# A token, scan and expert tower on one core: gathers into two PSUM banks a batch ahead, products of the powers spread over later batches, and another split of u among engines

## The chip, the cores and the metric

The kernel runs on one core of one Trainium2 chip. The metric is the device time in microseconds of one execution. The chip's engines work side by side, each through its own queue in order: TensorE (PE; its weight loads are shown apart as PEld) multiplies matrices into the eight banks of PSUM, VectorE (DVE) and ScalarE (ACT) read and write PSUM and SBUF, GpSimd (POOL) reads and writes SBUF only, and SyncE (SP) issues most of the DMAs. An engine waits for another through semaphores.

## The reference

Eight sequences of 512 ids go through three layers. The first looks every id up in a quantised table of 125 rows, applies a convolution of two taps along the sequence and a relu:

```
e = w_emb[clip(y, 0)];  h = relu(conv(pad(e), w, taps=2))
```

The second adds to h a linear recurrence over the normalised h (called u), with a 64x64 matrix A in four heads, written in the reference as an associative scan in log space; the states are divided by the largest of their row and go through C, and u through D:

```
u = layernorm(h);  x[t] = A x[t-1] + B u[t];  y = (e^2 * x / max|x|) C + u D;  h = h + y
```

The third is a layer norm, one matrix (attn_w), fc1, gelu, fc2, a last matrix and a gelu, with eight experts given by position:

```
x_attn = normed @ attn_w.T + attn_b + xf;  out = gelu(fc2(gelu(fc1(x_attn))) @ next_w.T + next_b);  h = h + out
```

## The kernel before

A batch is one sequence, 512 columns, held as 16 places in a chunk by 32 chunks, so that the scan is 16 steps inside chunks and a scan over the 32 chunks. Eight batches make two groups of four; the scan works on a group at a time.

The front is a loop over b = 0 to 9 that each engine writes out in its own order; all that the change touches lies in it. What it does for batch b:

- `spread_ids(b)` on TensorE copies the row of ids to all partitions of a bank; VectorE's `one_hot(b)` compares it with the row number; GpSimd's `edge(b)` copies the 31 columns at the chunks' edges, `onehot<-onehot` (L465).
- `gather(b)` (L1026 to L1038) is 16 matmuls of one-hot by table into bank 2, in four quarters; only the last quarter waits for `edge(b)`. From batch 1 on it waits for `h_ready` of the batch before, which frees the bank.
- ScalarE writes `h` of the batch from the bank with a relu (L590). VectorE takes its statistics, `st` and `mv` (L745, L749). GpSimd makes `rstd1` and `shift1` of them in four operations of which each waits for the one before (L480 to L483).
- The division (h - mean) * rstd gives `u`, in four pieces of 128 columns. `U_DVE` says how many of them VectorE does (L772); ScalarE does the others (L607). On both this stands one turn of the loop later than the batch's `h`.
- `transpose_u` on TensorE (L1047, four matmuls into bank 3) stands two turns later, and ScalarE's copy to `uT` (L595).

Beside it run the products of the powers of A. The list `prep` has seventeen of them, numbered 0 to 16; each is a matmul into bank 4 or 5 in turn (L986) and a copy by ScalarE (L555) to `pw`, `pw_t`, `late_b`, `pk` or `pk_t`, and most need the copy of the one or two before. `PREP_ROUND` says how many are issued in each turn: first ahead of the turn's transposition, then behind it.

In turns 6 and 7 the first group's run products come in, `run_piece(0, n)`: four of them into bank 6 (L1061, in turn 6) from `uT` of batches 0 to 3, and four into bank 7 (L1067, in turn 7) in three parts each, which need high and low parts of u. The high parts are ScalarE's `late_p`, `b_p` and four `u_first` (L579 to L582, the function `split_high`), the low parts are VectorE's (L755, L778, L779). ScalarE copies each four to `X` (L569). In turn 8 TensorE begins the scan over chunks with `ends` (L1080). Later work (the scan's carries, the mixer, the experts) follows in a written order that the change leaves alone.

Of the kernel before, what the change touches and what calls it, by code (L numbers as in the profile page):

```python
# [37 lines left out]
ACT = mybir.ActivationFunctionType  # L38
# [6 lines left out]
P = 128  # L45
NB = 8
# [4 lines left out]
GB = NB // NG  # L51
# [3 lines left out]
CH = 128  # L55
# [14 lines left out]
RUN = 4  # L70
# [4 lines left out]
OH_SLOTS = 4  # L75
# [15 lines left out]
PA, PA_N = spans(PA_COLS)  # L91
# [3 lines left out]
def build(nc, ids, emb, conv, pack_a, pack_b, fc1, fc2, out):  # L95
    with ExitStack() as ctx:
# [7 lines left out]
        pa = sb("pa", [P, PA_N])  # L104
# [15 lines left out]
        onehot = sb("onehot", [VOC, OH_SLOTS, EXT * NCH], BF16)  # L120
# [13 lines left out]
        scale_h = sb("scale_h", [P, 1])  # L134
        h = sb("h", [P, NB, NQ * CH])
# [37 lines left out]
        with ExitStack() as early:  # L173
# [13 lines left out]
            late_p = sb_early("late_p", [P, 2, (RUN - 1) * P], F32R)  # L187
            b_p = sb_early("b_p", [P, 2, NP * P], F32R)
# [5 lines left out]
        bank = [ctx.enter_context(nc.psum_tensor(f"bank{n}", [P, 512], F32)) for n in range(8)]  # L194
# [9 lines left out]
        scale_h_ready, oh_edge = sem("scale_h_ready"), sem("oh_edge")  # L204
# [6 lines left out]
        idb_done, oh_ready, gat_done, h_ready = sem("idb_done"), sem("oh_ready"), sem("gat_done"), sem("h_ready")  # L211
# [22 lines left out]
        b_hi, b_lo = sem("b_hi"), sem("b_lo")  # L234
# [15 lines left out]
        def late(a):  # L250
            return late_b[:, a].rearrange("p n m -> p (n m)")
# [60 lines left out]
        def ids_bank(b):  # L312
            return bank[{2: 3, 3: 6}.get(b, b % 2)][0:VOC, :]

        def scan_bank(a):
            return bank[6 + a][:]

# [3 lines left out]

        U_DVE = (2, 2, 2, 2, 2, 4, 4, 4)

        PREP_ROUND = ((1, 0), (1, 0), (1, 0), (1, 1), (1, 1), (1, 2), (1, 1), (1, 1), (1, 1), (1, 0))

        FUSED_FRONT = 3
        MIXER = 8
# [16 lines left out]

        assert sum(map(sum, PREP_ROUND)) == N_POW

        def prep_tasks(b, after):
            first = sum(map(sum, PREP_ROUND[:b])) + (PREP_ROUND[b][0] if after else 0)  # L350
            return range(first, first + PREP_ROUND[b][after])

        def numbered(plan):

# [53 lines left out]
        with nc.Block() as block:  # L408
# [131 lines left out]
            def _(act):  # L540
# [34 lines left out]
                    nc.scalar.activation(every_run(g, a, q + 1), scan_bank(a).rearrange("p (b r k) -> p b r k", b=GB, k=NCH),  # L575
                                         ACT.Copy).then_inc(x_ready[g], 1)

                def split_high():
                    nc.scalar.activation(late_p[:, 0], late(1), ACT.Copy).then_inc(b_hi, 1)  # L579
                    nc.scalar.activation(b_p[:, 0], pa[:, PA["b"]], ACT.Copy).then_inc(b_hi, 1)  # L580
                    for b in range(GB):
                        nc.scalar.activation(u_split(0, 0)[:, b], uT[:, b], ACT.Copy).then_inc(u_hi[0], 1)  # L582

                act.wait_ge(ld_pa, 32)
                for b in range(NB + 2):
                    if b < NB:
                        act.wait_ge(gat_done, b + 1)
                        if b == 0:
                            act.wait_ge(scale_h_ready, 1)
                        nc.scalar.activation(h[:, b, :], bank[2][:], ACT.Relu, scale=scale_h[:]).then_inc(h_ready, 1)  # L590
                    for t in prep_tasks(b, 0):
                        copy_out_prep(t)
                    if b >= 2:
                        act.wait_ge(u_t_done, b - 1)
                        nc.scalar.activation(uT[:, b - 2, :, :].rearrange("p i k -> p (i k)"), bank[3][:],  # L595
                                             ACT.Copy).then_inc(uT_ready, 1)
                    for t in prep_tasks(b, 1):
                        copy_out_prep(t)
                    if 1 <= b <= NB and U_DVE[b - 1] < NQ:
                        act.wait_ge(rstd1_ready, b)  # L600
                        if b == 1:
                            act.wait_ge(h_ready, 1)
                        if b >= 3:
                            act.wait_ge(u_t_done, b - 2)
                        for q in range(U_DVE[b - 1], NQ):
                            s = slice(q * CH, (q + 1) * CH)
                            last = nc.scalar.activation(u[:, (b - 1) % 2, s], h[:, b - 1, s], ACT.Identity,  # L607
                                                        scale=rstd1[:, b - 1, q:q + 1], bias=shift1[:, b - 1, q:q + 1])
                        last.then_inc(u_act_ready, 1)
                    if b == NB - 2:  # L610
                        split_high()
                    if b in (NB - 2, NB - 1):
                        copy_runs(0, b - (NB - 2))
                    if b >= NB:
                        copy_fused(b - NB)
# [32 lines left out]
                for j in range(-3, NB):  # L648
                    for n in range(8):
# [26 lines left out]
                        b = j + 1  # L676
# [8 lines left out]
                        b = j + 2  # L685
# [289 lines left out]
            def _(pe):  # L975
                mm = nc.tensor.matmul

                def prepare(t):
                    if t >= 2:
                        pe.wait_ge(prep_ready, t - 1)  # L980
                    dst = bank[4 + t % 2]
                    if t < N_POW:
                        out_, lhs, rhs, need = prep[t]
                        if need > max(t - 1, 0):
                            pe.wait_ge(prep_ready, need)
                        last = mm(dst[:, 0:out_.shape[1]], lhs, rhs, start=True, stop=True)  # L986
                    else:
                        pe.wait_ge(ld_pb, 16)
                        mm(dst[:, 0:1], pb[:, PB["attn"]], pa[:, PA["ln_b"]], start=True, stop=True)
                        mm(dst[:, 1:1 + NE], pb[:, PB["nw"]], pa[:, PA["fc2_b"]], start=True, stop=True)  # L990
                        pe.wait_ge(centre_ready, 1)
                        pe.wait_ge(attn_g_ready, 1)
                        last = mm(dst[:, P:P + CH], centre[:], attn_g[:], start=True, stop=True)
                    last.then_inc(prep_done, 1)
# [30 lines left out]

                def gather(b):  # L1026
                    pe.wait_ge(oh_ready, b + 1)
                    if b >= 1:
                        pe.wait_ge(h_ready, b)
                    for q in (1, 2, 3, 0):  # L1030
                        if q == 0:
                            pe.wait_ge(oh_edge, b + 1)
                        for n, (tap, part) in enumerate([(0, 0), (0, 1), (1, 0), (1, 1)]):

                            at = (q * TQ + tap) * NCH
                            last = mm(bank[2][:, q * CH:(q + 1) * CH], onehot[:, b % OH_SLOTS, at:at + P],  # L1036
                                      tab[:, part, tap, :], start=(n == 0), stop=(n == 3))
                    last.then_inc(gat_done, 1)  # L1038

# [10 lines left out]
                def run_piece(g, n):  # L1050
                    a, q = divmod(n, RUN)
                    if n == 0:
                        pe.wait_ge(uT_ready, GB * (g + 1))
                        pe.wait_ge(prep_ready, N_LATE)
                    if q == 0 and g == 1:
                        if a == 0:
                            pe.wait_ge(run_ready[0], 1)
                        else:
                            pe.wait_ge(x_ready[0], NP * (RUN - 1))
                    if a == 0:  # L1060
                        last = mm(scan_bank(a), b_then(a, RUN - 1 - q), u_runs(g, q), start=(q == 0), stop=(q == RUN - 1))  # L1061
                    else:
                        if q == 0:
                            pe.wait_ge(b_lo, 2)
                            pe.wait_ge(u_lo[g], GB)
                        for k, (w, m) in enumerate(PARTS):
                            last = mm(scan_bank(a), b_split(w, a, RUN - 1 - q), u_runs_split(g, m, q),  # L1067
                                      start=(q == 0 and k == 0), stop=(q == RUN - 1 and k == len(PARTS) - 1))
                    if q == RUN - 1:
                        last.then_inc(run_done[g], 1)  # L1070
# [86 lines left out]
                for b in range(NB + 2):  # L1157
                    if b == 0:
                        pe.wait_ge(tab_ready, 1)
                    if b < NB:  # L1160
                        gather(b)
                    if 3 < b + 3 < NB:
                        spread_ids(b + 3)
                    for t in prep_tasks(b, 0):
                        prepare(t)
                    if b >= 2:
                        transpose_u(b - 2)
                    for t in prep_tasks(b, 1):
                        prepare(t)
                    if b in (NB - 2, NB - 1):  # L1170
                        for q in range(RUN):
                            run_piece(0, (b - (NB - 2)) * RUN + q)
                    if b >= NB:
                        carry_step(0, b - NB)
                        fuse(b - NB)
# [206 lines left out]
```

## Time and profile before

| | us |
|---|---|
| median of 3 runs | 176.03 (176.02 to 176.11) |
| the profiled execution | 175.44 |
| its span, first to last instruction | 173.7 |
| PE busy / DVE / ACT / POOL | 162.0 / 134.7 / 97.7 / 100.5 |

The profile is of one execution. Its span is the time from its first to its last instruction; the rest of the execution's own 175.44 us lies around it. A timeline gives the start and the length of instructions from the span's start, with the idle time of the engine before them in brackets and what released it. A length counts until the result is written, so the next instruction of the same engine can start a little before it is over. For TensorE, float32 matmuls show as two records each.

### The profile page before, as it was taken

The page shows a single profiled execution, that of the slowest core. Times are in us where ns is not written, and L with a number is a line of the kernel's source. Part 1 is how long each engine was busy: PE and PEld are TensorE (multiplying, and loading weights), DVE is VectorE, ACT ScalarE, POOL GpSimd, SP SyncE. Part 2 cuts the span into 40 slices and gives each one's busy share as a digit, 9 for nine tenths or more (in the row PEclk, how much of TensorE's full clock was granted, in tenths as well). Part 3 has the DMA queues.
Part 4 walks back from the last instruction along what each step waited for, and adds up shares of the span by engine and source line. Part 5 has one row for each costly group of instructions (what it writes and reads, how often), then busy time and mean ns, then how long its engine had stood idle before and what let it go on. Part 6 is the DMA issues. An engine that isn't in the chain of part 4 may idle for free.

```text
span 173.7 us, 3449 instructions
## 1 busy us (share of the span) xinstructions
PE 162.0 (93%) x1149; PEld 137.3 (79%) x1149; DVE 134.7 (78%) x406; ACT 97.7 (56%) x227; POOL 100.5 (58%) x169
## 2 busy tenths in 40 slices
PE   5978999999999999988999989999999999998892
PEld 2666776885756799864679889999999999988891
DVE  3989779645355777999974998989979896668983
ACT  3149999441224241202335867859778597786691
POOL 5347769399993000400503593996969879698600
PEclk9999999999999999999999999999999999999999
DMA  4995000000000000000000000010010101001103
GB/s 147 398 430 213 4 2 0 0 6 0 0 0 0 4 0 0 0 6 0 0 0 0 0 4 0 0 66 0 11 55 0 60 0 54 12 2 64 55 5 121
DMA packets 2181, 7.46 MB, mean 43 GB/s; under 512 B 238, under 2 KB 748, under 8 KB 1908
## 3 DMA queue, kind: packets, MB, share of 16 engines
q1 hardware_dynamic: 2146, 7.23, 10.7%
q8 instruction: 9, 0.15, 0.4%
q14 instruction: 8, 0.07, 0.1%
q10 hardware_dynamic: 18, 0.02, 0.1%
HBM read 5.15 MB, written 2.10 MB: 42 GB/s over the span
## 4 chain that ended last, share of the span: by engine, by line
PE 71%; DVE 8%; POOL 7%; ACT 6%; issue 5%; DMA 1%; POOLq 0%; DVEq 0%; ACTq 0%
PE bank L1265 10%; PE bank L1285 10%; PE bank L1215 7%; PE bank L1130 6%; PE bank L1124 5%; PE bank L1061 4%; PE bank L1011 4%; PE bank L1212 4%; PE bank L1067 3%; PE bank L1235 3%; PE bank L1092 2%; POOL hid_p L523 2%; POOL rstd L506 2%; PE bank L986 2%; PE bank L1036 2%
## 5 line engine op out<-in xcount | busy, mean ns | idle before, releaser
L523 POOL TENSOR_TENSOR hid_p<-hid_f,hid_p 128x256 fp32r<-128x256 f32 x52 | 37.2, 741 | 17.2 <-ACT hid_p L667 15.6
L665 ACT ACTIVATE hid_f<-bank,pa 128x256 f32<-128x256 f32 x64 | 30.7, 487 | 17.5 <-PE bank L1265 15.8
L1265 PE MATMUL bank<-xaT_p,fc_p 128*128 128x256 f32 x192 | 34.9, 293 | 0.2 <-issue 0.2
L1285 PE MATMUL bank<-hid_p,out_hi 128*128 128x256 f32 x128 | 33.1, 293 | 1.5 <-POOL hid_p L523 1.1
L506 POOL TENSOR_TENSOR rstd<-spread,neg_half 128x8 f32<-128x8 f32 x8 | 13.2, 1646 | 30.7 <-DVE spread L916 30.7
L1265 PEld LDWEIGHTS bank<-xaT_p,fc_p 128*128 128x128 f32 x192 | 26.8, 190 | 0.3 <-issue 0.3
L1285 PEld LDWEIGHTS bank<-hid_p,out_hi 128*128 128x128 f32 x128 | 23.4, 188 | 3.5 <-POOL hid_p L523 2.3
L667 ACT ACTIVATE hid_p<-bank,pa 128x256 fp32r<-128x256 f32 x48 | 23.4, 487 | 0.0
L1215 PE MATMUL bank<-pb,xh 128*128 128x128 f32 x128 | 19.5, 276 | 0.0
L1285 PE MATMUL bank<-hid_p,out_lo 128*128 128x256 f32 x64 | 17.9, 279 | 0.0
L1215 PEld LDWEIGHTS bank<-pb,xh 128*128 128x128 f32 x128 | 16.9, 192 | 0.0
L745 DVE BATCH_NORM_STATS2 st<-h 128x6 f32<-128x128 f32 x64 | 13.9, 281 | 2.9 <-ACT h L590 2.6
L575 ACT ACTIVATE X<-bank 128x512 f32<-128x512 f32 x12 | 7.2, 598 | 14.0 <-PE bank L1130 14.0
L1212 PE MATMUL bank<-pb,uT 128*128 128x128 f32 x64 | 12.5, 276 | 0.5 <-DVE xh L940 0.5
L897 DVE SCALAR_TENSOR_TENSOR xaT_p<-bank,attn_c,xaT_p 128x256 fp32r<-128x256 f32 x16 | 7.0, 478 | 7.6 <-ACT xaT_p L681 7.6
L884 DVE TRANSPOSE_TENSOR_REDUCE amax<-X 128x16 f32<-128x512 f32 x16 | 10.4, 687 | 3.0 <-ACT X L575 3.0
L1130 PE MATMUL bank<-X,pa 128*128 128x512 f32 x24 | 12.3, 599 | 0.0
L1285 PEld LDWEIGHTS bank<-hid_p,out_lo 128*128 128x128 f32 x64 | 12.1, 189 | 0.0
L863 DVE SCALAR_TENSOR_TENSOR bank<-h,ratio,bank 128x128 f32<-128x128 f32 x32 | 9.0, 348 | 3.3 <-PE bank L1235 3.3
L1212 PEld LDWEIGHTS bank<-pb,uT 128*128 128x128 f32 x64 | 10.0, 191 | 1.5 <-DVE xh L940 0.9
L872 DVE TENSOR_SCALAR xa<-bank,rstd,shift 128x128 f32<-128x128 f32 x32 | 10.9, 403 | 0.3
L565 ACT ACTIVATE out_hi<-bank 128x512 fp32r<-128x512 f32 x8 | 4.8, 598 | 10.8 <-PE bank L1011 10.8
(154 smaller groups left out, 365.4 us busy)
## 6 DMA issues: line engine op xcount, KB each, us to landing
fc_w<-in_fc SPq DMA_DIRECT2D x2, 2048.0 KB, 11.4
out<-res SPq DMA_DIRECT2D x7, 256.0 KB, 2.0
pa<-in_pack_a SPq DMA_DIRECT2D x1, 407.0 KB, 3.1
pb<-in_pack_b SPq DMA_DIRECT2D x1, 384.0 KB, 4.9
out<-res SPq DMA_DIRECT2D x2, 128.0 KB, 1.7
pw<-in_pack_a SPq DMA_DIRECT2D x1, 64.0 KB, 3.1
emb_w<-in_emb SPq DMA_DIRECT2D x1, 62.5 KB
conv_w<-in_conv ACTq DMA_DIRECT2D x1, 1.0 KB
```

The costliest lines, as they stand in the source:

```text
L506: nc.gpsimd.tensor_tensor(rstd2[:, b, :, :].rearrange("p s q -> p (s q)"), spread2[:, b % 2, :, :].rearrange("p s q -> p (s q)"), neg_half[:],
L523: nc.gpsimd.tensor_tensor(hid_p[1][:, half, c, :], hid_f[:, m % HID_SLOTS, :], hid_p[0][:, half, c, :].bitcast(F32), ALU.subtract).then_in ...
L665: full = nc.scalar.activation(hid_f[:, m % HID_SLOTS, :], src, ACT.Gelu, bias=bias)
L667: nc.scalar.activation(hid_p[0][:, half, c, :], src, ACT.Gelu, bias=bias).then_inc(hid_ready, 1)
L745: last = nc.vector.bn_stats(st[:, b % 2, q, :], h[:, b, q * CH:(q + 1) * CH])
L872: last = nc.vector.tensor_scalar(xa[:, s], bank[4][:, s], rstd2[:, b, 1, q:q + 1], shift2[:, b % 2, q:q + 1], ALU.mult, ALU.subtract)
L884: last = nc.vector.tensor_reduce(amax[:, b % 2, a, :], X[g][:, a * GB + bb, 1:EXT, :], AX.X, ALU.max, apply_absolute_value=True, apply_tra ...
L1130: mm(scan_bank(a), a1, every_run(g, a, q), start=False, stop=True).then_inc(state_done[g], 1)
L1212: mm(dst, uT[:, b, q * TQ:(q + 1) * TQ, :].rearrange("p i k -> p (i k)"), pb[:, PB["d"]], start=True, stop=False)
L1215: last = mm(dst, xh[:, b % 2, a, q * P:(q + 1) * P], pb[:, PB["c"]][:, a * CH:(a + 1) * CH], start=False, stop=(a == NP - 1))
L1265: last = mm(fc1_bank(8 * b + n)[:, 0:HALF], fc1_p[w][:, e * HID + c * P:e * HID + (c + 1) * P], xaT_p[m][:, b % 2, half, :], start=(k == 0 ...
L1285: last = mm(out_bank(b, half)[:, half * HALF:(half + 1) * HALF], out_p[w][:, e, c * CH:(c + 1) * CH], hid_p[m][:, half, c, :], start=(c == ...
```

## The change

Gathers go into bank 2 for even and bank 7 for odd batches. In turn b TensorE issues the gather of b + 1 (turn 0: of 0 and 1), which waits for `h` of b - 1. Since bank 7 is also used early for the scale of h and later for the second four run products, gather 1 waits for `scale_h_ready` and the fifth run product for `h_ready` of all eight. `U_DVE` changes for batch 0 (VectorE 2 to 1 pieces) and batch 4 (2 to 4). `PREP_ROUND` has a third place: behind the third of a turn's four run products on TensorE, and on ScalarE between the second and the third `u_first` in turn 6.

```
-        U_DVE = (2, 2, 2, 2, 2, 4, 4, 4)
-        PREP_ROUND = ((1, 0), (1, 0), (1, 0), (1, 1), (1, 1), (1, 2), (1, 1), (1, 1), (1, 1), (1, 0))
+        U_DVE = (1, 2, 2, 2, 4, 4, 4, 4)
+        PREP_ROUND = ((1, 0, 0), (1, 0, 0), (1, 0, 0), (1, 1, 0), (1, 1, 0), (1, 0, 0), (1, 1, 1), (1, 1, 1), (1, 1, 0), (1, 0, 0))
+        def gather_bank(b):
+            return bank[(2, 7)[b % 2]]
...
# ScalarE
-                        nc.scalar.activation(h[:, b, :], bank[2][:], ACT.Relu, scale=scale_h[:]).then_inc(h_ready, 1)
+                        nc.scalar.activation(h[:, b, :], gather_bank(b)[:], ACT.Relu, scale=scale_h[:]).then_inc(h_ready, 1)
                     if b == NB - 2:
-                        split_high()
+                        split_high(range(GB // 2))
+                    for t in prep_tasks(b, 2):
+                        copy_out_prep(t)
+                    if b == NB - 2:
+                        split_high(range(GB // 2, GB))
# TensorE
                 def gather(b):
                     pe.wait_ge(oh_ready, b + 1)
-                    if b >= 1:
-                        pe.wait_ge(h_ready, b)
+                    if b == 1:
+                        pe.wait_ge(scale_h_ready, 1)
+                    if b >= 2:
+                        pe.wait_ge(h_ready, b - 1)
...
+                    if (g, n) == (0, RUN):
+                        pe.wait_ge(h_ready, NB)
...
                     if b == 0:
                         pe.wait_ge(tab_ready, 1)
-                    if b < NB:
-                        gather(b)
+                        gather(0)
+                    if b + 1 < NB:
+                        gather(b + 1)
...
                         for q in range(RUN):
                             run_piece(0, (b - (NB - 2)) * RUN + q)
+                            if q == RUN // 2:
+                                for t in prep_tasks(b, 2):
+                                    prepare(t)
```

TensorE, turns 6 and 7, before; the gathers are `bank2<-tab,onehot`, the run products write banks 6 and 7, the transpositions bank 3, the products of the powers banks 4 and 5:

```order
L986 MATMUL bank4<-pw,pw_t 128x256
L986 MATMUL bank5<-pw_t,pw 128x128
L1036 MATMUL bank2<-tab,onehot 128x128 x16
L986 MATMUL bank4<-pw,pw_t 128x128
L1047 MATMUL bank3<-ident_m,u 128x128 x4
L986 MATMUL bank5<-pw_t,pw 128x128
L1061 MATMUL bank6<-uT,late_b 128x512 x3
L1061 MATMUL bank6<-uT,pa 128x512
L1036 MATMUL bank2<-tab,onehot 128x128 x16
L986 MATMUL bank4<-pk,pk_t 128x128
L1047 MATMUL bank3<-ident_m,u 128x128 x4
L986 MATMUL bank5<-pk_t,pk 128x128
```

The same place now, from the last gather on:

```order
L1047 MATMUL bank7<-tab,onehot 128x128 x16
L995 MATMUL bank4<-pw,pw_t 128x256
L1058 MATMUL bank3<-ident_m,u 128x128 x4
L995 MATMUL bank5<-pw_t,pw 128x128
L1074 MATMUL bank6<-uT,late_b 128x512 x3
L995 MATMUL bank4<-pw,pw_t 128x128
L1074 MATMUL bank6<-uT,pa 128x512
L995 MATMUL bank5<-pw_t,pw 128x128
L1058 MATMUL bank3<-ident_m,u 128x128 x4
L995 MATMUL bank4<-pk,pk_t 128x128
L1080 MATMUL bank7<-u_first,late_p 128x512 x9
L995 MATMUL bank5<-pk_t,pk 128x128
```

Product 8 (`bank4<-pw,pw_t 128x256`) stands behind the gather of batch 7; product 10 stands behind three run products, product 11 ahead of the transposition of batch 5, and product 12 (`bank4<-pk,pk_t`) ahead of the second four run products, of which three have product 13 behind them. The gather of batch 7 has left its place behind the first four.

ScalarE in turns 6 and 7, before:

```order
L590 ACTIVATE h<-bank2,scale_h 128x512
L555 ACTIVATE pk<-bank4 128x128
L595 ACTIVATE uT<-bank3 128x512
L555 ACTIVATE pk_t<-bank5 128x128
L579 ACTIVATE late_p<-late_b 128x384
L580 ACTIVATE b_p<-pa 128x256
L582 ACTIVATE u_first<-uT 128x512 x4
L569 ACTIVATE X0<-bank6 128x4x4x32
L590 ACTIVATE h<-bank2,scale_h 128x512
L555 ACTIVATE pk<-bank4 128x128
```

ScalarE now, from the copy of product 8 on:

```order
L559 ACTIVATE pw<-bank4 128x256
L600 ACTIVATE uT<-bank3 128x512
L559 ACTIVATE pw_t<-bank5 128x128
L584 ACTIVATE late_p<-late_b 128x384
L585 ACTIVATE b_p<-pa 128x256
L587 ACTIVATE u_first<-uT 128x512 x2
L559 ACTIVATE pk<-bank4 128x128
L587 ACTIVATE u_first<-uT 128x512 x2
L573 ACTIVATE X0<-bank6 128x4x4x32
L595 ACTIVATE h<-bank7,scale_h 128x512
L559 ACTIVATE pk_t<-bank5 128x128
```

The copy of product 10 (`pk<-bank4`) has moved between the second and the third `u_first`, that of product 11 (`pk_t<-bank5`) behind `h` of batch 7. The place of `h` 7 behind `X0` is the same.

## Rows read from the trace of the kernel before

**Rows 1.** The page: busy time by engine, and the chain that ended last.
```profile
PE 162.0 (93%) x1149; PEld 137.3 (79%) x1149; DVE 134.7 (78%) x406; ACT 97.7 (56%) x227; POOL 100.5 (58%) x169
...
PE 71%; DVE 8%; POOL 7%; ACT 6%; issue 5%; DMA 1%; POOLq 0%; DVEq 0%; ACTq 0%
```

**Rows 2.** Busy us by stretch: PE, PEld, DVE, ACT, POOL; granted clock, DMA.
```profile
7.00:24.70 17.70, 15.24 (x161) 12.81 (x160) 14.57 (x66) 13.25 (x33) 11.67 (x34) 1.00 0.47 199
24.70:30.20 5.50, 5.46 (x35) 3.30 (x33) 5.47 (x20) 5.09 (x12) 4.29 (x5) 1.00 0.00 1
30.20:39.80 9.60, 8.79 (x56) 7.97 (x57) 5.50 (x20) 3.82 (x10) 6.56 (x11) 1.00 0.01 3
39.80:57.50 17.70, 17.70 (x71) 11.54 (x70) 8.62 (x15) 5.36 (x11) 13.23 (x15) 1.00 0.00 0
57.50:80.00 22.50, 21.57 (x143) 18.55 (x141) 19.85 (x51) 4.15 (x9) 2.21 (x4) 1.00 0.01 2
```

**Rows 3.** Waits, 7 to 40 us: total us, times, longest.
```profile
ACT h L590 <- PE bank L1036: 3.9, 3, 2.5
...
PE bank L1036 <- ACT h L590: 1.1, 2, 0.6
```

**Rows 4.** Timeline of ACT: start, length, instruction, idle before.
```profile
12.64 0.88 ACT L607 ACTIVATE u<-h,shift,rstd 128x128 f32<-128x128 f32 x2 [1.33 <-POOL shift L483]
13.42 0.67 ACT L590 ACTIVATE h<-bank,scale_h 128x512 f32<-128x512 f32 x1
...
26.05 2.18 ACT L582 ACTIVATE u_first<-uT 128x512 fp32r<-128x512 f32 x4
28.34 0.60 ACT L569 ACTIVATE X<-bank 128x512 f32<-128x512 f32 x1
29.24 0.69 ACT L590 ACTIVATE h<-bank,scale_h 128x512 f32<-128x512 f32 x1 [0.30 <-PE bank L1036]
```

**Rows 5.** Timeline of DVE: statistics of batches 2 and 6, u.
```profile
14.12 0.87 DVE L745 BATCH_NORM_STATS2 st<-h 128x6 f32<-128x128 f32 x4 [0.22 <-ACT h L590]
...
24.53 0.87 DVE L745 BATCH_NORM_STATS2 st<-h 128x6 f32<-128x128 f32 x4 [1.13 <-ACT h L590]
...
25.73 1.09 DVE L772 TENSOR_SCALAR u<-h,mv,rstd 128x128 f32<-128x128 f32 x4
26.73 0.55 DVE L778 TENSOR_TENSOR late_p<-late_b,late_p 128x384 fp32r<-128x384 f32 x1
```

**Rows 6.** Timeline of POOL: batches 0, 2, 4 and 6.
```profile
12.36 0.25 POOL L483 TENSOR_SCALAR shift<-tmp 128x4 f32<-128x4 f32 x1
12.54 0.21 POOL L465 COPY onehot<-onehot 125x31 bf16<-125x31 bf16 x1
...
15.49 0.23 POOL L480 TENSOR_SCALAR tmp<-mv 128x4 f32<-128x4 f32 x1 [0.54 <-DVE mv L749]
...
22.24 0.24 POOL L483 TENSOR_SCALAR shift<-tmp 128x4 f32<-128x4 f32 x1
...
24.42 0.20 POOL L482 TENSOR_TENSOR tmp<-mv,rstd 128x4 f32<-128x4 f32 x1
...
27.33 2.76 POOL L482 TENSOR_TENSOR tmp<-mv,rstd 128x4 f32<-128x4 f32 x1
```

**Rows 7.** Timeline of PE: transpositions, run products, gather 7, `ends`.
```profile
13.66 0.63 PE L1047 MATMUL bank<-ident_m,u 128*128 128x128 f32 x4 [0.68 <-ACT u L607]
...
24.02 0.63 PE L1047 MATMUL bank<-ident_m,u 128*128 128x128 f32 x4
...
24.70 2.74 PE L1061 MATMUL bank<-uT,late_b 128*128 128x512 f32 x6
...
28.14 1.06 PE L1036 MATMUL bank<-tab,onehot 125*128 125x128 bf16 x16
...
30.18 2.37 PE L1067 MATMUL bank<-u_first,late_p 128*128 128x512 f32 x9
...
33.97 1.49 PE L1080 MATMUL bank<-X,pw 128*128 128x248 f32 x6
```

More of the change, by code:

```diff
@@ L347, in build, with prep_tasks @@
         assert sum(map(sum, PREP_ROUND)) == N_POW
-        def prep_tasks(b, after):
-            first = sum(map(sum, PREP_ROUND[:b])) + (PREP_ROUND[b][0] if after else 0)
-            return range(first, first + PREP_ROUND[b][after])
+        def prep_tasks(b, place):
+            first = sum(map(sum, PREP_ROUND[:b])) + sum(PREP_ROUND[b][:place])
+            return range(first, first + PREP_ROUND[b][place])
         def numbered(plan):
@@ L576, in copy_state, with split_high @@
                                          ACT.Copy).then_inc(x_ready[g], 1)
[L578 to L581, printed above, removed]
+                def split_high(batches):
+                    if 0 in batches:
+                        nc.scalar.activation(late_p[:, 0], late(1), ACT.Copy).then_inc(b_hi, 1)
+                        nc.scalar.activation(b_p[:, 0], pa[:, PA["b"]], ACT.Copy).then_inc(b_hi, 1)
+                    for b in batches:
                         nc.scalar.activation(u_split(0, 0)[:, b], uT[:, b], ACT.Copy).then_inc(u_hi[0], 1)
@@ L1035, in gather @@
                             at = (q * TQ + tap) * NCH
-                            last = mm(bank[2][:, q * CH:(q + 1) * CH], onehot[:, b % OH_SLOTS, at:at + P],
+                            last = mm(gather_bank(b)[:, q * CH:(q + 1) * CH], onehot[:, b % OH_SLOTS, at:at + P],
                                       tab[:, part, tap, :], start=(n == 0), stop=(n == 3))
```

## The prediction

> **What bounds the kernel now.** I read the busy shares and the chain of waits first, then busy time by stretch, then the waits of the front by line, and then the four engines' timelines between 7 and 40 us. TensorE is busy 93% of the span and makes up 71% of the chain that ended last [rows 1]. By stretch, TensorE has 17.70 of 17.70 us busy between 39.8 and 57.5, but 15.24 of 17.70 between 7.0 and 24.7, and 8.79 of 9.60 between 30.2 and 39.8 [rows 2]. So before 24.7 us the kernel goes by a loop through other engines, and from there on by TensorE's queue. The change touches only what is issued up to about 38 us.
>
> The loop of the front is this: Pool's `shift1` of batch b, ScalarE's pieces of `u` of b, ScalarE's `h` of b+2, VectorE's statistics of b+2, Pool's `shift1` of b+2. At batch 0: shift1 ends at 12.36 + 0.25 = 12.61, ScalarE's two pieces of u start at 12.64, `h` of batch 2 at 13.42, the statistics start at 14.12 after a wait of 0.22 for that `h`, and Pool starts at 15.49 after 0.54 idle, waiting for them [rows 4 to 6]. The row to look at is what `h` waits for: in the whole stretch ScalarE waits for a gather three times, 3.9 us in all [rows 3]; those are batches 0, 1 and 7 (2.5 us is the first). For batches 2 to 6 the gather is done while ScalarE still works on u. TensorE waits for `h` twice, 1.1 us together, at the gathers of batches 1 and 2 [rows 3].
>
> **The change, part by part.** All starts below are in the time of the profiled execution, 175.44 us, whose span is 173.7.
>
> *Two banks, a batch ahead.* No instruction is added. TensorE's 1.1 us of waiting for `h` go. What they release is `h` of batch 1: product 0 of the powers now stands behind two gathers, so ScalarE's copy of it is done near 9.77 and `h` 1 starts there instead of at 10.45. Its statistics start no earlier, as VectorE has the one-hot of batch 4 first. Next late is the loop above, which holds no gather. New waits: the last four matmuls of gather 3 need Pool's edge copy of batch 3, at 12.54 to 12.75, since Pool has it behind the four operations of batch 0 [rows 6]. TensorE idles from about 11.4 to 12.87; behind it stand the ids row of batch 5, product 2 and the first transposition. The transposition needs u 0, and did at 13.66 [rows 7]; the one-hot of batch 5 starts near 13.53 instead of 13.16 and ends at 14.2, before VectorE's statistics can start (14.53, below). Priced at 0; without that cover it is 0.4 (13.53 less 13.16). Gather 1's wait for `scale_h` is over before it starts. Gather 7 (1.06 long, 0.89 to the next start) moves from behind the first four run products, 28.14 [rows 7], to about 22.2: TensorE has 0.89 less to issue there. Whether that is a gain depends on what the second four products wait for.
>
> *Split of u.* Batch 0 goes from two pieces on VectorE and two on ScalarE to one and three. A piece is 0.39 on ScalarE: (13.42 − 12.64) / 2 [rows 4]. So `h` 2 starts at 13.81. VectorE already waited for `h` there (0.22), and Pool for VectorE (0.54) [rows 5, 6], so all of it passes: statistics at 14.53, Pool at 15.90 instead of 15.49. Followed on through batches 3 and 4 with the same durations, the statistics of 3 start near 16.90, of 4 near 19.60, and `shift1` of batch 4 ends at 22.95, against 22.24 + 0.24 = 22.48 before [rows 6]. Bounds of this term: 0, if a slack that the rows don't show takes it, and 0.47; I take 0.44, which both chains below it give. Batch 4 goes wholly to VectorE: statistics of batch 5 end near 23.26, four pieces take 1.0 (25.73 to the next start; 1.09 long) [rows 5], so u 4 is ready at 24.34, where ScalarE's pair would have been ready at about 24.4. That swap is worth 0. The transposition of batch 4 starts at 24.46 instead of 24.02 [rows 7].
>
> *Products of the powers.* Seventeen of them as before; 8 and 9 leave batch 5, and 8 to 13 are spread over batches 6 and 7. The first run product starts at 24.46 + 0.44 + 0.22 (product 9) = 25.12. Each run product is 0.86: (28.14 − 24.70) / 4 [rows 7]. Product 10 now stands behind three of them: 25.12 + 2.58 = 27.70, written by 28.08. ScalarE's copy of product 10 stands between `u_first` 1 and 2. Without a wait ScalarE would get there at 26.05 + 0.44 + 2 × 0.53 = 27.55 (0.53 is the pitch of the four, (2.18 − 0.60) / 3 with 0.60 the length of such a 512-column copy) [rows 4]. It waits until 28.14: 0.59. The copy is 0.16 more. The other half of `u_first` is 1.06, so the copy of the runs (`X`) starts near 29.37, where it was 28.34 [rows 4].
>
> Then `h` 7, which stands behind `X` on ScalarE: 29.87, written at 30.56 (0.69 long). It started at 29.24 before [rows 4]. Here a new wait counts: the fifth run product writes bank 7, which gather 7 filled, so it may not start before `h` 7 is done: 30.70. Behind `h` 7 stands the copy of product 11, to 30.72, and product 12, which needs it, stands on TensorE before the fifth run product: start 30.86, plus 0.22, so the second four run products start at 31.08 instead of 30.18 [rows 7]. That is +0.90. VectorE's low parts, the old release, would be ready near 30.3.
>
> Product 13 (0.22) now lies inside these four instead of behind them; ScalarE's copy of the second runs waits for the fourth, and `ends` for that copy, while what TensorE has in between (two products and a transposition, 0.88) is shorter than the copy's 0.04 + 0.60 + 0.14. `ends` starts at 35.1 instead of 33.97 [rows 7].
>
> The sum of what each adds to the lateness: 0.44 (u), 0.59 and 0.16 (the wait and the copy within `u_first`), less 0.17 that `X` waited before for its run product (26.05 + 4 × 0.53 = 28.17 against 28.34), which makes the 1.03 of `X`; less 0.13, as the second four run products stand 31.08 − 29.37 = 1.71 behind `X` where it was 1.84; and 0.2 for product 13. **+1.1 us**. The gather taken out, 0.89, is inside the comparison: TensorE stands idle for longer than that, from about 29.5 to 30.86.
>
> Behind `ends` nothing has changed in kind or order, and TensorE had no idle time from 39.8 to 57.5 [rows 2], so I let the delay pass whole to the end. That makes 176.5 in the profiled execution's time. The median of the runs is 176.03, 0.59 above it, so **177.1**.
>
> The Trainium skill has a rule that speaks the other way: Perfetto Trace Analysis, section "Matmuls", says that independent matmul groups should rotate through different PSUM banks so that the evacuation of one overlaps the matmuls of the next. Taken as the whole answer it would give back the waits of TensorE for `h`; the trace shows those waits, 1.1 us, but not on the loop that sets the pace, so it is a rival below and not in the sum.
>
> **The rivals.** *Faster: the two banks pay.* TensorE's 1.1 us before gathers 1 and 2 [rows 3] come off the path and gather 7's place adds nothing: 176.03 − 1.1 = 174.9, up to 0.9 less still if TensorE's queue alone held 24 to 30 us. For it: TensorE is busy 5.46 of 5.50 us there [rows 2]. Against it: `h` of batches 2 to 6 doesn't wait for gathers [rows 3], and 1.13 us of VectorE's wait for `h` 6 ends with ScalarE's u pieces [rows 5], not with a gather. 8%.
>
> *No change.* The extra u piece is swallowed and ScalarE's wait at product 10 is covered because the second four run products wait for VectorE anyway: low parts of `u_first` at 30.3 give +0.1, and product 13 another +0.2, 176.3; with half of the u piece swallowed too, 176.1. Against it: two further gates (`h` 7 and product 12) stand later than VectorE. 10%.
>
> *Slower, by more.* TensorE's idle time at gather 3, about 1.5 us, is longer than any in the front now (0.68 before the first transposition [rows 7]); what is queued behind it costs VectorE 0.4 too (above), and Pool's short multiply, which took 2.76 us instead of 0.20 once VectorE worked on `u_first` [rows 6], meets batch 6 again or also batch 5. With 0.4 and a part of the 2.56: 177.5 to 178.5. The granted clock was 1.00 in every stretch [rows 2]; should it fall to its other level in the new pause, the gathers behind it would cost this much too. 10%.
>
> *Only a part is real:* the split and `X` order cost 0.4 to 0.7 and the rest is found again later as TensorE's queue has slack behind 57.5 us (21.57 of 22.50 busy [rows 2]): 176.5 to 176.7. It shares the forecast's side. 17%. The forecast itself, 176.8 to 177.4: 55%.
>
> **How the numbers follow.** 0.2% of this time is 0.35 us, what a measurement can tell from nothing. Faster: 8%. Within it: 10%. Slower: 82%, the other three cases. The range leaves out the fast rival and the tail of the slow one: 176.2 to 177.8.
>
> **What would show it.** In the changed kernel: ScalarE's three u pieces at 12.64 and `h` 2 at 13.8; VectorE's statistics of batch 2 at 14.5; gather 3 cut in two with a wait for Pool near 12.9; a wait of 0.5 to 0.6 on ScalarE in `u_first`; `X` at 29.3 to 29.5 followed at once by `h` 7; TensorE idle above 1 us before product 12, released by ScalarE's copy `pk_t`; `ends` near 35.1. The forecast is wrong if `h` 2 starts at 13.4, if the second four run products start before 30.4, or if `ends` is 1.1 late and the span is not.

## The result, and the profile after

| | before | after |
|---|---|---|
| median of 5 runs, us | 176.03 (175.97 to 176.15) | 176.82 (176.57 to 176.97) |
| the profiled execution | 175.44 | 176.81 |
| its span | 173.7 | 175.0 |

The ratio is 1.0049, with a 95% interval of 1.0029 to 1.0069: slower by 0.8 us, between 0.5 and 1.2. The page of the kernel after, its busy shares and chain, reads almost as [rows 1], with 0.3 us more of TensorE, 2.5 us less of Pool, and TensorE's share of the chain down from 71% to 67% (Pool's is up from 7% to 9%):

```profile
PE 162.3 (93%) x1149; PEld 137.3 (78%) x1149; DVE 134.7 (77%) x407; ACT 97.5 (56%) x226; POOL 98.0 (56%) x169
...
PE 67%; POOL 9%; DVE 8%; ACT 6%; issue 5%; DMA 2%; POOLq 1%; ACTq 0%; DVEq 0%
```

TensorE's waits over the whole span of the kernel after, by line:

```profile
PE bank L995 <- ACT pk_t L559: 1.2, 1, 1.2
...
PE bank L1047 <- POOL onehot L469: 1.1, 1, 1.1
```

The two waits for `h` of [rows 3], 1.1 us together, are gone, and in their place stand two new ones of 1.2 and 1.1 us: for ScalarE's copy of product 11, and for Pool's edge copy. The timelines of the kernel after, ScalarE first:

```profile
9.23 0.69 ACT L595 ACTIVATE h<-bank,scale_h 128x512 f32<-128x512 f32 x1 [3.17 <-PE bank L1047]
...
13.34 1.26 ACT L612 ACTIVATE u<-h,shift,rstd 128x128 f32<-128x128 f32 x3 [1.28 <-POOL shift L487]
14.51 0.67 ACT L595 ACTIVATE h<-bank,scale_h 128x512 f32<-128x512 f32 x1
...
27.10 1.15 ACT L587 ACTIVATE u_first<-uT 128x512 fp32r<-128x512 f32 x2
28.76 0.28 ACT L559 ACTIVATE pk<-bank 128x128 f32<-128x128 f32 x1 [0.51 <-PE bank L995]
28.93 1.14 ACT L587 ACTIVATE u_first<-uT 128x512 fp32r<-128x512 f32 x2
29.97 0.59 ACT L573 ACTIVATE X<-bank 128x512 f32<-128x512 f32 x1
30.45 0.69 ACT L595 ACTIVATE h<-bank,scale_h 128x512 f32<-128x512 f32 x1
31.02 0.28 ACT L559 ACTIVATE pk_t<-bank 128x128 f32<-128x128 f32 x1
```

TensorE:

```profile
7.22 2.91 PE L1047 MATMUL bank<-tab,onehot 125*128 125x128 bf16 x32
...
13.51 0.40 PE L1047 MATMUL bank<-tab,onehot 125*128 125x128 bf16 x4 [1.10 <-POOL onehot L469]
...
25.04 0.66 PE L1058 MATMUL bank<-ident_m,u 128*128 128x128 f32 x4 [0.39 <-DVE u L781]
...
31.45 0.46 PE L995 MATMUL bank<-pk,pk_t 128*128 128x128 f32 x2 [1.21 <-ACT pk_t L559]
31.66 2.37 PE L1080 MATMUL bank<-u_first,late_p 128*128 128x512 f32 x9
...
35.67 1.49 PE L1093 MATMUL bank<-X,pw 128*128 128x248 f32 x6
```

VectorE's last result, in the kernel before and after:

```profile
171.01 0.43 DVE L956 TENSOR_TENSOR res<-gel,hT 128x256 f32<-128x256 f32 x1 [0.65 <-ACT gel L643]
...
172.36 0.43 DVE L965 TENSOR_TENSOR res<-gel,hT 128x256 f32<-128x256 f32 x1 [0.65 <-ACT gel L652]
```

Compared as they stand, the first `h` of ScalarE is 0.70 late already (9.23 against 8.53). The first experiment shows that this is chance, and all profiles together bear it out: the first `h` starts between 8.49 and 9.32 in the five with one bank and between 8.48 and 9.50 in the nine with two. So from here on I count from the start of the first `h` in each execution. Then `h` of batch 2 starts at 5.28 (before 4.89), the transposition of batch 4 at 15.81 (15.49), `X` at 20.74 (19.81), the second four run products at 22.43 (31.66 less 9.23; before 21.65) and `ends` at 26.44 (25.44). The last result is written at 163.56 (172.36 + 0.43 less 9.23) against 162.91, and I call this the end. So `ends` is 1.00 late, and the end only 0.65. Where the rest went is seen in VectorE's and Pool's timeline behind `ends`. Before:

```profile
37.80 1.07 DVE L821 TENSOR_SCALAR attn_g<-pb,pa 128x128 f32<-128x128 f32 x1
38.79 0.63 DVE L823 TENSOR_SCALAR centre<-ident_m 128x128 f32<-128x128 f32 x1
...
37.52 1.27 POOL L492 TENSOR_TENSOR fc_p<-fc_w,fc_p 128x512 fp32r<-128x512 f32 x1
...
39.48 0.49 PE L993 MATMUL bank<-attn_g,centre 128*128 128x128 f32 x2 [0.81 <-DVE centre L823]
```

After:

```profile
39.50 0.57 DVE L830 TENSOR_SCALAR attn_g<-pb,pa 128x128 f32<-128x128 f32 x1
40.00 0.63 DVE L832 TENSOR_SCALAR centre<-ident_m 128x128 f32<-128x128 f32 x1
...
38.72 1.27 POOL L496 TENSOR_TENSOR fc_p<-fc_w,fc_p 128x512 fp32r<-128x512 f32 x1
...
40.68 0.49 PE L1002 MATMUL bank<-attn_g,centre 128*128 128x128 f32 x2 [0.31 <-DVE centre L832]
```

The same operation takes 1.07 in one kernel and 0.57 in the other, and in both it ends 0.08 behind Pool's subtraction: 37.52 + 1.27 = 38.79 and 38.87; 38.72 + 1.27 = 39.99 and 40.07. TensorE waits for its successor `centre`. So at this place TensorE goes by Pool, and Pool was only 0.51 late: its first `fc_p` started 26.38 behind the first `h` before (34.91) and 26.89 after (36.12). TensorE's matmul there is 0.50 late (31.45 against 30.95), its wait 0.31 instead of 0.81. Pool starts its first `fc_p` behind VectorE's `u` of batch 7, which is 0.51 late as well (25.30 against 24.79).

From there on TensorE is 0.50 late until 65.5 us behind the first `h`, where an addition of VectorE waits 0.18 that did not wait before, and the 0.50 becomes the 0.65 of the end. The same step is there in e1 (0.37 to 0.53); what brings it about was not tried. VectorE before and after:

```profile
74.00 0.42 DVE L799 TENSOR_TENSOR X<-X,bank 128x256 f32<-128x256 f32 x1
...
75.36 0.42 DVE L808 TENSOR_TENSOR X<-X,bank 128x256 f32<-128x256 f32 x1 [0.18 <-DVE bank L942]
```

### The profile page after: what moved, and what is told of

It is laid out like the page before. It is cut to its first block, busy times and chain, and to the rows that moved or that the text cites. A ratio compares the mean times of both kernels' runs of the same rounds, so it can differ in the third digit from the quotient of the medians.

```text
span 175.0 us, 3448 instructions
## 1 busy us (share of the span) xinstructions
PE 162.3 (93%) x1149; PEld 137.3 (78%) x1149; DVE 134.7 (77%) x407; ACT 97.5 (56%) x226; POOL 98.0 (56%) x169
## 4 chain that ended last, share of the span: by engine, by line
PE 67%; POOL 9%; DVE 8%; ACT 6%; issue 5%; DMA 2%; POOLq 1%; ACTq 0%; DVEq 0%
PE bank L1302 9%; PE bank L1282 9%; PE bank L1232 7%; PE bank L1143 6%; PE bank L1137 5%; PE bank L1020 4%; PE bank L1229 4%; PE bank L1074 3%; POOL hid_p L527 3%; PE bank L1080 3%; PE bank L1252 3%; PE bank L1105 2%; POOL rstd L510 2%; ACT h L595 2%; DMA ids_i<-in_ids 2%
## 5 line engine op out<-in xcount | busy, mean ns | idle before, releaser
L1047 PEld LDWEIGHTS bank<-tab,onehot 125*128 125x128 bf16 x128 | 8.6, 106 | 2.9 <-POOL onehot L469 1.6
```

## The experiments

All are counted from the start of the first `h` in the profiled execution. "Late" is against the kernel before (25.44 for `ends`, 162.91 for the end). The times of one kernel's runs spread by 0.4 to 2.1 us, so the medians decide only the larger distances. The counted times of two executions of the kernel before agree to 0.03 from batch 4 on and to 0.06 at the end.

| kernel | median, us | before, beside it | ratio, 95% interval | `ends` | end |
|---|---|---|---|---|---|
| before again (e0) | 176.09, one run | 175.99 | | 25.44 | 162.97 |
| split alone (e1) | 176.45 | 175.99 | 1.0024 (1.0011 to 1.0036) | 25.76 | 163.47 |
| banks alone (e2) | 175.86 | 175.99 | 0.9998 (0.9984 to 1.0013) | 25.44 | 162.89 |
| banks and split (e3) | 176.25 | 175.99 | 1.0013 (0.9999 to 1.0027) | 25.29 | 162.97 |
| banks and spread (e4) | 175.87 | 176.11 | 0.9999 (0.9973 to 1.0025) | 25.58 | 162.60 |
| all three (after) | 176.82 | 176.03 | 1.0049 (1.0029 to 1.0069) | 26.44 | 163.56 |
| before, centre early (e5) | 175.21 | 176.11 | 0.9944 (0.9928 to 0.9960) | 25.45 | 162.00 |
| after, centre early (e6) | 176.21 | 176.11 | 1.0002 (0.9989 to 1.0014) | 26.47 | 163.11 |
| after, product 12 late (e7) | 176.65 | 176.11 | 1.0022 (1.0008 to 1.0037) | 26.23 | 163.61 |
| two banks, best (e8) | 174.76 | 176.19 | 0.9925 (0.9903 to 0.9947) | 24.90 | 161.37 |
| after, batch 0 back (e9) | 176.38 | 176.19 | 1.0010 (0.9989 to 1.0031) | 26.79 | 163.77 |
| the same again (e12) | 176.98 | 176.24 | 1.0032 (1.0010 to 1.0054) | 26.09 | 163.09 |
| one bank, best (e13) | 175.10 | 176.24 | 0.9944 (0.9926 to 0.9962) | 25.37 | 161.94 |

**e0, the kernel before once more.** No edit.

> The kernel before, unchanged, for a second look at its front. In the two profiles so far TensorE's first gather was done 0.70 us later in the changed kernel (ScalarE's first h at 9.23 against 8.53). Theory C (chance of the single execution: when the ids land and when the first matmuls come to their short pitch): a second profile of the kernel before shows its first h at another time, between 8.5 and 9.3, and its own time near 176.0. Theory G (the second gather behind the first is the cause): its first h is again at 8.5.

Theory C. Its first gather and first `h`:

```profile
7.11 1.91 PE L1036 MATMUL bank<-tab,onehot 125*128 125x128 bf16 x16
...
9.11 0.69 ACT L590 ACTIVATE h<-bank,scale_h 128x512 f32<-128x512 f32 x1 [2.93 <-PE bank L1036]
```

The same 16 matmuls took 1.47 in the first profile of this kernel and 1.05 in later batches, and `h` started at 8.53 there. Behind it the counted times of `h` 1 and `h` 3 still differ (by 0.29 and 0.16); those of `h` 2 and of everything from batch 4 on to the matmul at `centre` agree to 0.03. The first profile was an early one: 175.44, with medians of 176.0 to 176.2 in all comparisons.

**e1 to e4, the three parts.** The edits are the tables alone, in the kernel before (e1) or after (e2 to e4):

```
e1  +U_DVE = (1, 2, 2, 2, 4, 4, 4, 4)
e2  +U_DVE = (2, 2, 2, 2, 2, 4, 4, 4)   and PREP_ROUND as before with a third place of 0
e3  PREP_ROUND as before with a third place of 0
e4  +U_DVE = (2, 2, 2, 2, 2, 4, 4, 4)
```

> The kernel before with the new split of u alone (1, 2, 2, 2, 4, 4, 4, 4). Theory A (the replay of the front): h of batch 2 0.39 late behind ScalarE's third piece, the transposition of batch 4 0.3 late, ends 0.2 late: 176.0 plus 0.2. Rival theory S (the split is the whole of the loss): plus 0.8.

> Gathers into two banks a batch ahead alone, with the split and the places of the products of before. Theory A: gathers were hidden behind ScalarE's work, so nothing is won; ends moves by 0.0 to 0.1: 176.0 to 176.1. Rival G (a second gather behind the first delays the first h, or the idle at gather 3 costs): plus 0.4 or more. Rival F (the waits for h were on the path): minus 1.

> The changed kernel without the spreading of the products (banks and split as changed, products as before, so u_first is one block of four again). Theory A: the wait and copy within u_first and product 12's wait go, and the second four run products start when VectorE's low parts are there: minus 0.15 against the kernel before at ends, so 175.8 to 176.0. If instead the loss lies in split or banks, it stays at 176.5 or above.

> The changed kernel with the split of u of before (banks and spread products stay). Counted from the first h of ScalarE to the same event, which leaves out when the ids land. Theory A (the replay): the transposition of batch 4 no longer late (before: 15.5 behind the first h), even 0.4 early as no product stands ahead of it; the second four run products at +0.1, ends at +0.3. Rival S2 (split and spread add up as 0.35 + 0.65): ends at +0.65.

Split alone: `h` of batch 2 at 5.29 (0.40 late), the transposition of batch 4 0.35 late, `ends` 0.32 late, where 0.2 was expected; the runs say 0.1% to 0.4% slower. It is part of the loss and not the whole. Banks alone: `ends` and the times of `h` 2 to 6 are the kernel's before to 0.02; `h` 1 starts 0.63 earlier, `h` 7 0.40 and the transposition of batch 5 0.94, and none of the three moves `ends`. Neither rival G nor F holds. Banks and split together: `ends` at −0.15, to the digit, though the end is at +0.06 and the median of 176.25 above the 175.8 to 176.0 that was expected. In this pair ScalarE does no piece of u 4 and finds gather 6 done, so `h` 6 starts 0.39 earlier (14.90 against 15.29), VectorE's low parts of `u_first` are done at 21.36 instead of 21.50, and gather 7 no longer stands in TensorE's queue; `h` 7 ends at 21.36 too. TensorE, e3:

```profile
30.28 1.94 PEld L1080 LDWEIGHTS bank<-u_first,late_p 128*128 128x128 f32 x9 [0.64 <-ACT h L595]
...
34.09 1.49 PE L1093 MATMUL bank<-X,pw 128*128 128x248 f32 x6
```

Banks and spread: `ends` +0.14 where 0.3 was expected, the end −0.31, as Pool (its first `fc_p` at 26.04, 0.34 early) and not `ends` sets the place of `centre`. So the parts do not add: 0.00 for the banks, −0.15 with the split, +0.14 with the spread, +1.00 with both. The transposition of batch 4 tells why. In e4 it stands at 14.97, half a microsecond early. The expectation put that down to the product ahead of it on TensorE; the rows show another reason. It waits for ScalarE's two pieces of u 4, and those start at 14.00 instead of 14.52, because the copies of products 8 and 9 no longer stand ahead of them. ScalarE before and in e4:

```profile
22.61 0.38 ACT L555 ACTIVATE pw<-bank 128x256 f32<-128x256 f32 x1 [0.23 <-PE bank L986]
22.89 0.27 ACT L555 ACTIVATE pw_t<-bank 128x128 f32<-128x128 f32 x1
23.05 0.87 ACT L607 ACTIVATE u<-h,shift,rstd 128x128 f32<-128x128 f32 x2
...
22.77 0.88 ACT L612 ACTIVATE u<-h,shift,rstd 128x128 f32<-128x128 f32 x2
```

That half microsecond pays for the wait within `u_first`, which is there in e4 as well:

```profile
27.43 0.28 ACT L559 ACTIVATE pk<-bank 128x128 f32<-128x128 f32 x1 [0.51 <-PE bank L995]
...
28.64 0.59 ACT L573 ACTIVATE X<-bank 128x512 f32<-128x512 f32 x1
```

With the new split the transposition waits for VectorE's four pieces of u (0.39 in the kernel after), which are done at 15.75, and stands at 15.81; the 0.5 is gone and the wait stays.

**e5 and e6, what TensorE's wait for `centre` is worth**, in the kernels before and after:

```
                 for n in range(1 + LEVELS + RUNS):
-                    if n == 2:
+                    if n == 0:
                         dve.wait_ge(ld_pb, 16)
```

> The kernel before with VectorE's two operations attn_g and centre moved ahead of the scan's first addition, into VectorE's idle time before ends; nothing else. Theory B (these two tie TensorE to Pool: attn_g waits until Pool's two-input operation is done, and TensorE waits 0.8 for centre): TensorE's wait goes and everything behind it comes 0.7 to 0.8 earlier, time minus 0.7. Theory A' (the delay passes whole and centre is only a step on TensorE's own chain): minus 0.1 to minus 0.3, since another wait stands right behind it.

> The changed kernel with the same move of attn_g and centre. Theory B: it wins only the 0.3 that TensorE waits there, and so stands 1.0 above the kernel before with the same move (e5), which is what ends is late: the half that was given back in the changed kernel was only this wait. Rival: it wins as much as in the kernel before, and the distance stays 0.5 to 0.8.

VectorE and TensorE in e5:

```profile
34.33 0.28 DVE L821 TENSOR_SCALAR attn_g<-pb,pa 128x128 f32<-128x128 f32 x1
34.52 0.22 DVE L823 TENSOR_SCALAR centre<-ident_m 128x128 f32<-128x128 f32 x1
...
38.27 0.37 PE L990 MATMUL bank<-pa,pb 128*128 128x8 f32 x2
38.49 0.47 PE L993 MATMUL bank<-attn_g,centre 128*128 128x128 f32 x2
```

The two take 0.28 and 0.22 there, before Pool begins. TensorE's matmul stands 0.95 earlier (30.00 against 30.95). That is the wait of 0.81, counted from the end of the matmul ahead of it, and 0.15 by which it now starts before that one is written (38.27 + 0.37 = 38.64 against 38.49). The end comes 0.91 earlier. The kernel after wins 0.45. The distance at the end is 163.11 − 162.00 = 1.11, and 1.00 between the medians, where `ends` is 1.02 apart. Theory B: the delay of the change is the full 1.0, and the kernel before loses half of it in a wait of its own.

**e7, product 12.** The kernel after with

```
-PREP_ROUND = (..., (1, 1, 1), (1, 1, 1), (1, 1, 0), (1, 0, 0))
+PREP_ROUND = (..., (1, 1, 1), (1, 0, 2), (1, 1, 0), (1, 0, 0))
```

> The changed kernel with product 12 moved behind the third of the second four run products, so that they no longer wait for it. Theory A: they start when h of batch 7 has left bank 7, 0.15 after its end, which is 0.4 earlier than in the changed kernel; as products 12 and 13 then both stand inside, ends comes only 0.15 to 0.2 earlier. Rival (the low parts of u_first are the gate): the four start 0.8 earlier. Rival (product 12 costs nothing): no change.

```profile
30.24 0.69 ACT L595 ACTIVATE h<-bank,scale_h 128x512 f32<-128x512 f32 x1
...
30.99 2.39 PE L1080 MATMUL bank<-u_first,late_p 128*128 128x512 f32 x9 [0.95 <-ACT h L595]
```

The four start 0.06 behind the end of `h` 7 and 0.45 earlier than in the kernel after (21.98 against 22.43); `ends` 0.21 earlier, the end not at all (163.61), since Pool still holds `centre`. Both gates are real and stand one behind the other: `h` 7, which frees bank 7, and product 12.

**e9 and e12, batch 0 given back to both engines.**

```
-U_DVE = (1, 2, 2, 2, 4, 4, 4, 4)
+U_DVE = (2, 2, 2, 2, 4, 4, 4, 4)
```

> The changed kernel with batch 0 split as before (2 and 2), batch 4 still wholly on VectorE. Theory A: h of batch 2 is on time again (4.89 behind the first h, not 5.28) and ends is 0.34 earlier than in the changed kernel, 26.1 behind the first h; the other half of what the split costs together with the spread products (1.00 against 0.14) stays, as the transposition of batch 4 waits for VectorE's four pieces. Rival: the third piece of batch 0 is the whole of it, ends at 25.6.

The first execution missed: `ends` at 26.79. TensorE shows another reason than the split:

```profile
7.50 2.77 PE L1047 MATMUL bank<-tab,onehot 125*128 125x128 bf16 x24
...
7.50 3.62 PE L1047 MATMUL bank<-tab,onehot 125*128 125x128 bf16 x32
```

The first row counts the matmuls of the two first gathers that had begun by about 10 us, the second all of them: the last 8 took 0.85, which is 0.106 each, where a later gather has 0.89 / 16 = 0.056. The first two gathers ended near 11.1, the one-hot of batch 4 waited 1.14 and the statistics of batch 1 began 1.00 late (3.81 against 2.81). So I ran it again.

> The kernel of e9 once more, as its profiled execution had both first gathers at 107 ns a matmul (normally the pitch falls to 56 within the first one), which made the one-hot of batch 4 and with it the statistics of batch 1 late. Theory A: in an execution where the first h is at 9.3 or earlier, ends is 26.1 behind the first h. Rival (the third piece is the whole): 25.6. Rival (it costs nothing): 26.4.

First `h` at 8.54, `ends` at 26.09. Giving batch 0 back wins 0.35 of the 0.86 that the split costs on top of banks and spread (26.44 − 25.58); the rest, 0.51, belongs to batch 4 on VectorE: the transposition of batch 4 stands at 15.46 in e12 and at 14.97 in e4. The medians of the two, 176.38 and 176.98, are too far apart to add anything.

**e8 and e13, the better version.** Both have `U_DVE = (2, 2, 2, 2, 4, 4, 4, 4)`, the products placed as before and `centre` early as in e5; e8 has the two banks, e13 one.

> Gathers into two banks a batch ahead, products as before, u split (2, 2, 2, 2, 4, 4, 4, 4), that is only batch 4 goes wholly to VectorE, and attn_g and centre moved ahead of the scan's first addition. Theory A with B: the third ScalarE piece of batch 0 (0.39) is gone, VectorE takes batch 4's, which lets ScalarE come to u_first earlier, ends 0.4 to 0.5 ahead of the kernel before (25.44 behind the first h), and the wait for centre is gone (0.96). Time 174.6 to 175.0, below e5 (175.2). Rival: the split's second part doesn't pay either, and it equals e5.

> The best version without the second bank: the kernel before with u split (2, 2, 2, 2, 4, 4, 4, 4) and with attn_g and centre moved as in e5. Theory A (the two banks pay only by taking gather 7 out from between the two fours of run products, once the low parts of u_first come earlier): ends 25.3 behind the first h, against 24.90 with two banks (e8) and 25.45 (e5); time 175.0 to 175.1, 0.3 above e8. Rival (the banks are worth nothing): it equals e8.

e8 beats both kernels: 174.76, 0.75% below the kernel before (0.5% to 1.0%), 161.37 counted. e13 comes to 175.10 and 161.94. The intervals of the two overlap, so their distance rests on the counted times of one execution each. TensorE in e8:

```profile
28.61 0.38 PE L995 MATMUL bank<-pk,pk_t 128*128 128x128 f32 x2
28.83 0.60 PE L1058 MATMUL bank<-ident_m,u 128*128 128x128 f32 x4
29.27 0.39 PE L995 MATMUL bank<-pk_t,pk 128*128 128x128 f32 x2
30.14 2.36 PE L1080 MATMUL bank<-u_first,late_p 128*128 128x512 f32 x9 [0.48 <-DVE u_first L764]
```

ScalarE's `h` of batch 6 in e13 and in e8:

```profile
23.76 0.69 ACT L590 ACTIVATE h<-bank,scale_h 128x512 f32<-128x512 f32 x1 [0.56 <-PE bank L1036]
...
23.54 0.69 ACT L595 ACTIVATE h<-bank,scale_h 128x512 f32<-128x512 f32 x1
```

Here the low parts of `u_first` are the gate of the second four in both. The second bank is worth 25.37 − 24.90 = 0.47 at `ends`, and it takes both things that it does. First, with u 4 wholly on VectorE ScalarE comes early to `h` 6. With one bank it then waits 0.56 for gather 6 and starts at 15.21; with two it starts at 14.52, and the low parts are done at 20.96 instead of 21.42. Second, with one bank gather 7 and the products behind it keep TensorE until 21.44 (21.22 and 0.22 for the last product), so early low parts alone would have won only about 0.13 (21.57 − 21.44, an estimate from these rows). The expectation of e13 had named the second and not the first. The change had this gain and covered it.

## Why the prediction was right, and where it was not

Forecast 177.1 (176.2 to 177.8), measured 176.82. By its own steps:

- *h of batch 2 0.39 late, behind the third piece:* 0.39 (and 0.40 in e1). Shown. The passing of it to the transposition of batch 4 was put at 0.44 and is 0.32.
- *Batch 4 wholly on VectorE: "That swap is worth 0":* wrong. The working compared VectorE's four pieces with a pair of ScalarE at about 24.4, but with products 8 and 9 gone from batch 5 that pair comes half a microsecond earlier (e4). The swap costs 0.51 (e12 against e4). The sum did not suffer, since it never counted the half microsecond as won; in that it was lucky.
- *Two banks: nothing won, 0 for the wait at gather 3:* shown by e2. The wait was 1.10 (1.20 in e2), not 1.5, and cost nothing. The Trainium skill's rule on rotating banks (Perfetto Trace Analysis, "Matmuls") gives nothing where ScalarE comes late to a gather that is done (e2, 0.00); where ScalarE comes early and waits 0.56 for gather 6, the overlap is part of a gain of 0.47 (e8 against e13).
- *Wait within `u_first`, 0.59, and the copy of 0.16:* 0.51 and 0.17. `X` 0.93 late, forecast 1.03.
- *Gates of the second four: low parts, then `h` 7, then product 12; 0.90 late:* 0.78, with the gates in that order (e7). What happens when product 12 goes was expected to 0.05 (e7: 0.45, expected 0.4).
- *`ends` 1.1 late:* 1.00.
- *Behind `ends` "I let the delay pass whole to the end":* this step failed. 0.50 was left at `centre` and 0.65 at the end. (The prediction named this itself as a sign of being wrong: `ends` 1.1 late and the span not.) I had read that TensorE has no idle time from 39.8 on, and had not asked of the 0.8 idle just ahead of it, which stands in [rows 2] as 8.79 of 9.60, what it hangs on. It hangs on Pool through VectorE, and Pool's lateness is that of u 7 and not of `ends`: 0.51 measured. By the prediction's own times `h` 7 starts 0.63 late (29.87 against 29.24), so the sum would have been about 0.6. Against its 1.1 stand 0.65 at the counted end and 0.79 between the medians.
- *The place of the profiled execution:* I added its distance to the median, 0.59, without asking where it lay. e0 shows that it lay in the first gather (`h` 0.58 later, the run 0.65 longer), which was quick in that one execution. That had no effect on the difference, but two profiles compared as they stand would have shown 1.3 for a change of 0.6 to 0.8.

The 0.65 of the counted times and the 0.8 of the medians agree within the interval (0.5 to 1.2). Whether the two gathers in a row make the first stretch longer on average, which would be the rest, stays open: with both ahead, a slow start also delays what stands behind gather 1 (e9), but e2's median, 0.13 below the kernel before, shows no such cost.

## What to carry to other kernels

Before a second buffer is given to a producer, look at what its consumer waits for: if the consumer comes late to data that is ready, the buffer wins nothing by itself, and what is freed is only the producer's place in its queue. If another edit lets the consumer come early, look again: then the two belong together (e3, e8). Operations put into the gaps of an engine's block (here a copy between four `u_first`) bring their own producer's lateness into the block, so each needs a check that its input is there at that time, after all the other edits of the change. And a delay does not pass whole: at every wait further on, ask which engine ends it and how late that engine is.

## What the runs showed of the hardware that I had not expected

VectorE's `tensor_scalar` of `attn_g` took 0.28 with Pool idle (e5) and 1.07 when it started inside a two-input float32 operation of Pool, ending 0.08 behind it; started later inside the same operation in the kernel after, it took 0.57 and ended 0.08 behind as well. In all ten profiles where it keeps its old place it took between 0.57 and 1.18 and ended 0.08 or 0.09 behind Pool's. The Trainium skill's GPSIMD Engine Reference, in its table ahead of "Terminology", says that the two share SBUF interfaces and contend when VectorE's instruction is in a two-port mode or has two SBUF inputs; the rows agree that they contend, though they do not show the mode of `attn_g`, and in these ten VectorE was done only behind the whole of Pool's operation. The other way round, Pool's multiply of batch 6 took 2.76 [rows 6] when it started inside VectorE's `b_p` subtraction, ending 0.06 behind VectorE's block of `u_first` (30.09 against 30.03). In the kernel after it took 0.20, though it started inside the `late_p` subtraction just ahead (27.70, with `late_p` from 27.25 to 27.81). All 14 profiles divide so, seven and seven: about 2.75 inside `b_p`, 0.20 inside `late_p`. Why one of them holds Pool and the other does not is not shown.

The first gather's 16 matmuls took 1.47, 1.91 and more in different executions of the same instructions, at 0.106 us each to begin with, against 0.056 later. The rows print a granted clock of 1.00 for that stretch, but this is no measurement: the packed traces have no entry of the clock before the matmuls get quick. Their first entry, of the full level, stands at 7.82 us in the kernel before, 10.57 in e0, 9.23 in the kernel after and 11.19 in e9. In 13 of the 14 profiles the slow pitch ends within 0.1 of that entry, and in e9 the entry lies between the last slow gather and the first quick one. As 0.106 is nearly twice 0.056, and the entries know two levels, 1.0 and 0.5, the slow start is most likely the lower level; no entry shows it. What sets the moment of the rise is not shown. It moves whole executions by half a microsecond and more, and is the largest part of the spread of the runs that I can see.
